# One-hot building moved from GpSimd to VectorE, and ScalarE's next-block work moved ahead of its copy-out, in the edge loop of a graph block

## The reference, cut to what matters

```
tpw = h @ W_mlp4 ; w1, w2, w3, w4 = split(tpw, 4)        # per edge, 4 x 128
s0 = x0[sender]; s1 = x1[sender]                         # gather: 128 and 128 x 3
y0 = edge_attrs[:, 0:1]; y1 = edge_attrs[:, 1:4]
p1 = w1 * s0 * y0
p2 = (w2 * s0)[:, :, None] * y1[:, None, :]
p3 = w3[:, :, None] * s1 * y0[:, None, :]
p4 = w4 * einsum('eum,em->eu', s1, y1) / sqrt(3)
msg = segment_sum([p1, p4, p2, p3], receiver)            # into 1250 nodes
```

## Time and profile before

| | |
|---|---|
| median of 3 runs | 2287.73 us |
| span of the profiled execution, first to last instruction | 2276.7 us |
| median less span, which lies around the instructions | 11.0 us |
| PE busy | 2070.7 us, 91% |
| DVE busy | 1327.4 us, 58% |
| ACT busy | 1048.6 us, 46% |
| POOL busy | 644.0 us, 28% |

### The profile page before, as it was taken

The page is one execution under the profiler, slowest core; times in us unless marked ns, Lnnn a source line. Parts: engine busy times, 40 slices in busy tenths (PEclk is TensorE's granted clock), DMA queues, the critical chain, the costliest instruction groups (busy, mean ns, idle before and its releaser), DMA issues.

```text
span 2276.7 us, 45135 instructions
## 1 busy us (share of the span) xinstructions
PE 2070.7 (91%) x13564; PEld 1492.6 (66%) x13565; DVE 1327.4 (58%) x2831; ACT 1048.6 (46%) x2327; POOL 644.0 (28%) x759
## 2 busy tenths in 40 slices
PE   7899798888888887889999999999599999989998
PEld 4444343334343335678888888888478888778886
DVE  3212788888888887745565555555622257454444
ACT  6531333333333332267776777767243222454443
POOL 2102677777777777210000000001300000210000
PEclk9999999999999999799999999999899999989999
DMA  6642566666666668554701440032710110220000
GB/s 216 224 163 79 148 187 182 178 177 183 179 177 178 174 178 303 190 211 167 297 34 34 156 169 18 18 123 83 256 57 10 40 62 19 74 74 10 10 10 18
DMA packets 157293, 288.53 MB, mean 127 GB/s; under 512 B 43534, under 2 KB 85271, under 8 KB 152616
## 3 DMA queue, kind: packets, MB, share of 16 engines
q1 hardware_dynamic: 111349, 158.80, 20.4%
q0 software_dynamic: 37552, 121.91, 18.4%
q10 hardware_dynamic: 8322, 6.89, 0.9%
HBM read 233.69 MB, written 53.85 MB: 126 GB/s over the span
## 4 chain that ended last, share of the span: by engine, by line
PE 61%; issue 13%; DVE 8%; POOL 5%; DMA 5%; ACT 3%; another core or an unknown queue 1%; DVEq 1%; POOLq 1%; SPq 1%; ACTq 1%; PEldq 0%
PE psum L2580 14%; PE psum L2719 6%; PE psum L2752 4%; PE psum L2625 4%; PE psum L2570 4%; PE psum L2571 3%; PE psum L2572 3%; POOL big_b L1049 3%; PE psum L2616 3%; PE psum L2656 3%; PE psum L2646 2%; DMA big_b<-sender_table,wide 2%; PE psum L2298 2%; DVE big_b L1744 1%; PE psum L2670 1%
## 5 line engine op out<-in xcount | busy, mean ns | idle before, releaser
L1049 POOL DMA_INDIRECT big_b<-sender_table,wide x360 | 367.9, 1022 | 152.2 <-issue 85.0
L2429 PEld LDWEIGHTS psum<-big_b,wide 128*32 128x32 f32 x3600 | 169.7, 111 | 208.5 <-issue 111.9
L2429 PE MATMUL psum<-big_b,wide 128*32 128x256 f32 (+2 forms) x3600 | 279.6, 398 | 5.8 <-POOL wide L1079 5.6
L2580 PEld LDWEIGHTS psum<-xn_T,big_b 128*128 128x128 f32 x2048 | 261.9, 191 | 21.2 <-issue 3.2
L2399 PE MATMUL psum<-w_mlp,wide 64*128 64x512 f32 x728 | 211.3, 658 | 69.0 <-DVE big_b L1745 45.5
L2580 PE MATMUL psum<-xn_T,big_b 128*128 128x128 f32 x2048 | 265.0, 275 | 0.0
L1266 ACT ACTIVATE wide<-psum 128x384 f32<-128x384 f32 x45 | 22.1, 491 | 414.4 <-PE psum L2440 229.8
L1921 DVE TENSOR_TENSOR w_lo<-wide,w_hi 128x512 fp32r<-128x512 f32 x184 | 127.3, 692 | 117.9 <-ACT w_hi L1357 117.9
L2570 PE MATMUL psum<-w_hi,hid_hi 128*128 128x512 f32 x368 | 175.7, 478 | 12.1 <-DVE w_lo L1921 7.2
L1743 DVE TENSOR_TENSOR big_b<-psum,big_b 128x512 f32<-128x512 f32 x180 | 124.2, 690 | 97.2 <-DMA big_b<-sender_table,wide 76.9
L1259 ACT ACTIVATE wide<-wide 128x290 bf16<-128x290 f32 x360 | 158.6, 527 | 42.0 <-PEq L2402 37.2
(11 more groups left out here) (460 smaller groups left out, 3975.2 us busy)
## 6 DMA issues: line engine op xcount, KB each, us to landing
big_a<-in_L_ffn_W SPq DMA_DIRECT2D x12, 2048.0 KB, 12.4
big_b<-in_L_ffn_W SPq DMA_DIRECT2D x12, 2048.0 KB, 13.5
wide<-in_L_ffn_W SPq DMA_DIRECT2D x8, 2048.0 KB, 23.5
wide<-edge_hidden SPq DMA_DIRECT2D x182, 64.0 KB
edge_hidden<-wide SPq DMA_DIRECT2D x21, 512.0 KB, 3.0
tokens_sorted<-zeros SPq DMA_DIRECT2D x29, 256.0 KB
adj_dram<-big_a SPq DMA_DIRECT2D x1, 6400.0 KB, 22.4
xn_T<-tokens_sorted POOLq DMA_DIRECT2D x25, 256.0 KB, 2.9
```

Of the source, the lines that this page charges most:

```text
L1049: nc.gpsimd.indirect_dma_start(out=sent[q][:, j, :], out_offset=None, in_=sender_table, in_offset=bass.IndirectOffsetOnAxis(ap=indices[j], ...
L2429: nc.tensor.matmul(msg_psum[k].rearrange("p (c u) -> p c u", u=MUL)[bands[g], cols, :], hot_y[q][:, j, y, :], p[:, of, :], start=False, st ...
L2580: last = nc.tensor.matmul(psum[:, f % UP_BANKS, 0:P], ew1[a][:, c, f * P:f * P + P], tile_T[:, c, :], start=(c == 0), stop=(c == C - 1))
```

## The change

Three things change in the edge loop.

- **`hot_y` on VectorE.** `hot` and POOL's multiplication go. For each of the two groups DVE executes one `scalar_tensor_tensor`: (node numbers == receiver) * y, 128 partitions x 4 x 32 elements. Its output takes the place of both. DVE also sets the semaphore `hot_y_ready`.
- **GpSimd only gathers.** Its waits for `hot_low` and for the scatter of four steps earlier go with the multiplication.
- **ScalarE's order.** For block b+1 the `hot_step` pairs now stand ahead of the copy-out of block b, whose stores follow at once. The last step number of each block is kept in a register for the copy-out's wait.

```diff
-        hot = [edge_space2.take(2 * GRAIN)... for q in range(HALVES)]
...
                     for q in range(HALVES):
                         ahead = (q + 2) % HALVES
-                        pool.wait_ge(hot_low_ready, s * 4 + q + 5)
-                        pool.wait_ge(scatter_done, s * 4 + q + 1)
-                        pool.sem_inc(loop_entered, 1)
-                        nc.gpsimd.tensor_tensor(hot_y[q], hot[q].unsqueeze(2).to_broadcast([P, 2, Y, GRAIN]),
-                                                record[q][:, :, 0:Y].unsqueeze(3).to_broadcast([P, 2, Y, GRAIN]), ALU.mult)\
-                            .then_inc(hot_y_ready, 1)
                         pool.wait_ge(record_loaded[ahead], s * 16 + (q + 2) // HALVES * 16)
                         pool.wait_ge(products_done, s * 4 + q + 3)
...
                         last.then_inc(step_ready, 1)
-                return s
-
-            def block_flush(i, k, s):
+                act.reg_mov(last_unit[k], s)
+
+            def block_flush(i, k):
+                s = act.snap(last_unit[k], min_val=1, max_val=NB * EDGE_UNITS)
...
             block_start(0, 0)
-            s = block_steps_of(0, 0)
+            block_steps_of(0, 0)
             block_start(1, 1)
-            block_flush(0, 0, s)
             router_loads()
             with act.Fori(0, NB // 2 - 1) as i:
-                s = block_steps_of(i * 2 + 1, 1)
+                block_steps_of(i * 2 + 1, 1)
+                block_flush(i, 0)
                 block_store(i * 2, 0)
                 block_start(i * 2 + 2, 0)
-                block_flush(i, 1, s)
-                s = block_steps_of(i * 2 + 2, 0)
+                block_steps_of(i * 2 + 2, 0)
+                block_flush(i, 1)
                 block_store(i * 2 + 1, 1)
                 block_start(i * 2 + 3, 1)
-                block_flush(i + 1, 0, s)
...
                         dve.wait_ge(record_loaded[q], s * 16)
-                        dve.wait_ge(hot_y_ready, s * 4 + q + 1)
                         dve.wait_ge(scatter_done, s * 4 + q + 1)
                         nodes = iota_nodes[:, bass.ds(b * BLOCK, GRAIN)]
-                        nc.vector.tensor_tensor(hot[q], nodes.unsqueeze(1).to_broadcast([P, 2, GRAIN]),
-                                                record[q][:, :, Y:Y + 1].to_broadcast([P, 2, GRAIN]), ALU.is_equal)
+                        for j in range(2):
+                            last = nc.vector.scalar_tensor_tensor(hot_y[q][:, j, :, :], nodes.unsqueeze(1).to_broadcast([P, Y, GRAIN]),
+                                                                  record[q][:, j, Y:Y + 1],
+                                                                  record[q][:, j, 0:Y].unsqueeze(2).to_broadcast([P, Y, GRAIN]),
+                                                                  ALU.is_equal, ALU.mult)
+                        last.then_inc(hot_y_ready, 1)
```

More of the change, by code:

```diff
@@ L264, in graph_block_kernel @@
         record = [edge_space2.take(2 * REC).rearrange("p (j k) -> p j k", j=2) for q in range(HALVES)]
-        hot = [edge_space2.take(2 * GRAIN).rearrange("p (j n) -> p j n", j=2) for q in range(HALVES)]
         hot_y = [edge_space2.take(2 * Y * GRAIN).rearrange("p (j y n) -> p j y n", j=2, y=Y) for q in range(HALVES)]
@@ L1060, in _ @@
                 gather(q, [src_ids[:, j:j + 1] for j in range(2)])
-            pool.sem_inc(hot_y_ready, 8)
             for q in range(2):
@@ L1243, in _ @@
             units = act.alloc_register("act_units")
+            last_unit = [act.alloc_register(f"act_last_unit{k}") for k in range(2)]
             def block_start(b, k):
@@ L1280, in _ @@
             block_start(0, 0)
-            s = block_steps_of(0, 0)
+            block_steps_of(0, 0)
             block_start(1, 1)
-            block_flush(0, 0, s)
             router_loads()
             with act.Fori(0, NB // 2 - 1) as i:
-                s = block_steps_of(i * 2 + 1, 1)
+                block_steps_of(i * 2 + 1, 1)
+                block_flush(i, 0)
                 block_store(i * 2, 0)
                 block_start(i * 2 + 2, 0)
-                block_flush(i, 1, s)
-                s = block_steps_of(i * 2 + 2, 0)
+                block_steps_of(i * 2 + 2, 0)
+                block_flush(i, 1)
                 block_store(i * 2 + 1, 1)
                 block_start(i * 2 + 3, 1)
-                block_flush(i + 1, 0, s)
-            s = block_steps_of(NB - 2, 1)
+            block_steps_of(NB - 2, 1)
+            block_flush(NB // 2 - 1, 0)
             block_store(NB - 3, 0)
             block_start(NB - 1, 0)
-            block_flush(NB // 2 - 1, 1, s)
-            s = block_steps_of(NB - 1, 0)
+            block_steps_of(NB - 1, 0)
+            block_flush(NB // 2 - 1, 1)
             block_store(NB - 2, 1)
-            block_flush(NB // 2, 0, s)
+            block_flush(NB // 2, 0)
             block_store(NB - 1, 0)
+            s = act.snap(last_unit[0], min_val=1, max_val=NB * EDGE_UNITS)
             for q in range(2):
@@ L1706, in _ @@
                 front(front_slots.get((n, 2), []))
+            dve.sem_inc(hot_y_ready, 8)
             dve.sem_inc(hot_low_ready, 8)
```

## The result

| | before | after |
|---|---|---|
| median | 2286.15 us (4 runs, 2284.14 to 2292.48) | 2331.98 us (4 runs, 2326.20 to 2343.21) |
| span of the profiled execution | 2276.7 us | 2328.0 us |
| granted clock over the edge loop | 0.97 | 0.94 |

The account below looks back on a forecast made before the run. A round of waits bounded the edge loop; after the change DVE would: 179 x 3.19 + 44 x 0.36 = 587 us, plus 7, 594 against 635.8. Forecast 2246 us, 8 in 10 between 2230 and 2273.

Parts of the forecast that it names:

- The price of the one-hots: DVE in the edge loop: each new instruction costs 0.27 us, so the step grows by 0.40 to 3.19 us.
- the sum: Edge loop: 179 x 3.19 + 44 x 0.36 = 587 us, including 72 us of new DVE work.
- The lock between DVE and POOL: Two-input DVE instructions are held during POOL's multiplication, 0.63 instead of 0.22 us, but not beside a gather.
- rival C: Edge loop: gathers hold the new DVE instructions, 0.41 us each time; 2303 us at 140 steps, 2320 in all; chance 0.10.
- A gather may now go as soon as its record is there and the products of four steps earlier are done: POOL in the edge loop: waits for `hot_low` and the scatter go; its round falls from 3.15 to at most 2.67 us.
- 3.4 us of slack, so the round no longer decides: Edge loop: rows arrive 9.4 us after the one-hots, DVE wants them after 12.8, so DVE decides.
- The 9.4 us: Slot-to-slot round from the one-hots: 0.5 us for SP's issue, record 3.9, gathers and landing 4.95.
- Cost: nothing: ACT's later copy-out and earlier `hot_step` stay covered; if the cover were gone, 0.84 us per block, 38 us.
- The clock: PE's granted clock, 0.97 over the loop: fewer long idle times give a small gain inside the 42 us.
- What lies around the span: 11.0 us added around the 2235 us span to give 2246, making the profiled execution equal to the median.
- B: Edge loop: the round still decides in part, a quarter of DVE's 97.2 us idle stays; 2270 us (2260 to 2281); chance 0.14.
- D: Another unseen wait of the same size replaces the removed one; time within 0.3% of 2288 us; chance 0.06.

Follow-up runs that it names:

- e3: The changed kernel with POOL's wait for `hot_low` put back ahead of each pair of gathers; 2248.81 us, ratio 0.9828 to the kernel before.
- e6: The changed kernel with gathers waiting for the products of three steps earlier, not four, and no wait for `hot_low`; 2256.06 us, ratio 0.9820.
- e4: The changed kernel with a multiplication of constants, of the old size, on POOL ahead of each pair of gathers, without the old waits; 2296.01 us, ratio 0.9962.
- e9: e3 with the gathers of two steps issued together, four on every other step, each with its own waits; 2284.82 us, ratio 0.9966.
- e1: The kernel before with ACT's new order and nothing else; 2245.56 us, ratio 0.9818.
- e20: e3 with each step's record load issued ahead of its hidden-activation load on SP; 2254.07 us, ratio 0.9821.
- e2: The changed kernel with ACT's old order; 2497.14 us, ratio 1.0929 to the kernel before.
- e17: The changed kernel with each step's record load issued ahead of its hidden-activation load on SP; 2333.22 us, ratio 1.0168.
- e11: The changed kernel with a 0.11 us memset (128x1) on POOL ahead of each pair of gathers; 2354.94 us, ratio 1.0254.
- e19: The changed kernel with POOL's gathers waiting for the products of this very step; 2411.56 us, ratio 1.0506.

## Why the prediction was wrong

**The price of the one-hots: right.** 3.18 us a step against 3.19 said. The new work on DVE is 49.8 us in busy time, less than the 72 us of the sum, probably since held and waiting ends of the removed instructions went with it.

**The lock between DVE and POOL: right.** No tail beside gathers, so rival C is dead.

**"A gather may now go as soon as its record is there and the products of four steps earlier are done": this is the step that failed.** I took a dropped wait for a relief that can only help. It is the whole loss. With that wait back (e3) the kernel takes 2249 us, against 2246 predicted; with the wait for the products moved by one step instead (e6), 2256, and the two can't be told apart by their ratios. The other terms thus held to about 11 us: e3's loop is 606.8 us against 596. That the time comes within 3 us is part luck, since the span of before was of a quick execution. The dropped wait never showed as time, and the earlier trace rows have no line for it, and so I priced it at nothing. In its place the runs showed this: without it POOL issues five to nine gathers in a row 20 times, in such stretches the queues of PE and SP crawl, and DVE stands 95.7 us, not for gathered rows but for PE's weights. That the wait's return ends it is shown; that the long runs of gathers bring it about is the likely reading.

**"3.4 us of slack, so the round no longer decides": wrong as used.** The 9.4 us were one turn of the earlier trace rows, in a kernel in which POOL was held back, and they allow 0.5 us for SP, which in the stretch above took 7.3 us for its register instructions alone. In the changed kernel DVE idles 95.7 us. With all of it, the sum of the prediction is 587 + 96 = 683 us, and 686.2 were measured.

**"Cost: nothing" for ACT's order: right, but it hid the gain.** ACT's order is the part that pays, 42 us alone. I had spread the gain over all three edits and so did not see that one gives it and the other two have to earn their 50 us.

**The clock.** A small gain was forecast; it fell from 0.97 to 0.94, as PE idles after the stalls. In e3 it is 1.00.

**What lies around the span.** I had 11.0 us. The profiled execution of after took 2329.8 us for a span of 2328.0, so 1.8 lie around it, and that of before must have been some 9 us quicker than the median. This changes nothing of the verdict.

**The rivals.** B had the right place in part (SP's queue holds the records, DVE idles 30 us and more) and the right rule ("from 42 us on nothing is gained"), but its idle time was to be for gathers. It was capped at a quarter of the idle time, for no reason but that two waits would go, and it had no slower end. With all 97 us its own sum would have read 691 us and 2343. D said what happened, "another wait of the same size" in the place of the one removed (95.7 us for 97.2), but priced it at no change and forgot the 50 us of new work that the wait no longer pays for. The slower side was given to C alone, by a mechanism that isn't there.

**What is shown and what isn't.** Shown: dropping the wait causes the loss; its size changes with the place where a gather may go; DVE idles for PE's weights; neither bytes nor the place of the records on SP are the cause. Not shown: what makes the queues of PE and SP crawl, and whether long runs of gathers set it off or the early gather itself. For the runs speak e4, where pairs alone leave 1.0 us of idle time, and the count of PE's slow steps below. e9 speaks against them in part, with 36 slow steps and no run over seven. No kernel here has early gathers in pairs with nothing else changed on DVE, which would decide it.

## What to carry to other kernels

A wait that costs nothing in the profile may still pace a queue. Before dropping one along with the instruction that it guarded, keep it in a second version, and try its credit one step to either side; here 3.2 us of distance were worth 3.8% of the time, and 2.3 us too many cost 6.8%. Where a change has several parts, time them one by one: no kernel here beats e1, which has only one of the three (ratio 0.9818; e3, e6 and e20, with 0.9828 to 0.9821, can't be told from it). Where an engine gets new work on the strength of its idle time, that time has first to be shown to go; if it stays, the new work costs in full.

## What the runs showed of the hardware

- TensorE's queue can run slow while the engine waits for nobody: single matmuls 1.4 us apart for 5.7 us (523.15 to 528.84). Counted from the records, weight loads of the loop that come after 1.20 to 1.45 us of idle "issue" time are 46 in after, 73 in e2, 37 in e17, 36 in e9 and 50 in e11, all with much "remote" idle time on DVE, but 12 before, 4 in e1, 2 in e3, 8 in e6 and 6 in e19. Of the 46 in after, 27 lie in runs of six gathers or more and 1 in a run of four. Their cause is open.
- SyncE's queue crawls almost only beside indirect DMAs. Its instructions of 0.6 to 0.8 us in the loop are 85 before, 156 in after, 157 in e1 and 67 in e3. All but 7 of after's begin inside a gather or within 0.31 us of its end, and all of the other three kernels'. These times are 75, 68, 79 and 79% of their loops. Since the fast e1 has as many as after, their number alone costs nothing.
- An indirect DMA of 128 rows holds POOL for 1.0 us, and a run of them goes at one each 1.30 us, whether a row has 2 KB or 512 B.
- An engine can wait for a matmul's semaphore long after the profile's modelled end of that matmul: 7.8 us in the piece of 528.98 (521.18 to 528.96). The release then has no name ("remote").
- `scalar_tensor_tensor` of 128 elements costs 0.265 us in a row of two, and it is not held beside a gather, but up to 1174 ns beside a GpSimd multiplication.
